# Turning the second expert's rows with VectorE and an exchange of quadrants, in the expert stage of an attention and mixture-of-experts layer

## The reference, cut to what matters

```python
buf = zeros(E * CAP + 1, H).at[slot].set(x[tok])      # E = 32 experts, CAP = 512 rows each
xe = buf[:E * CAP].reshape(E, CAP, H)                 # H = 256
gu = einsum('ech,eoh->eco', xe, gate_up_proj)         # 128 gate and 128 up columns
g, u = minimum(gu[..., :I], 7), clip(gu[..., I:], -7, 7)
h = silu(g) * u
ye = einsum('eci,ehi->ech', h, down_proj)             # gathered later, eight rows a token
```

## Time and profile before

| | |
|---|---|
| median of 3 runs | 3135.45 us (3132.16 to 3135.75) |
| the profiled execution's own time | 3129.23 us |
| its span, from first to last instruction | 3127.6 us |
| expert stage: first transpose to the first scores of the attention | 555.3 to 764.5 us |
| PE busy over the span | 98% |
| mean granted TensorE clock | 0.995 of full speed |

### The profile page before, as it was taken

The page is one execution under the profiler, slowest core; times in us unless marked ns, Lnnn a source line. Parts: engine busy times, 40 slices in busy tenths (PEclk is TensorE's granted clock), DMA queues, the critical chain, the costliest instruction groups (busy, mean ns, idle before and its releaser), DMA issues.

```text
span 3127.6 us, 54519 instructions
## 1 busy us (share of the span) xinstructions
PE 3068.8 (98%) x13443; PEld 1592.7 (51%) x13444; DVE 2624.5 (84%) x2773; ACT 1963.5 (63%) x3797; POOL 2102.4 (67%) x2156
## 2 busy tenths in 40 slices
PE   8999999999899999999999999999999999999998
PEld 3355444555455555555555555555555555555554
DVE  9622444334999999999999999999999999999995
ACT  5511420334677777777777777777777777777775
POOL 5877773011577777777777777777777777777776
PEclk9999999999999999999999999999999999999999
DMA  9821887665888888898888888988898888888887
GB/s 350 331 88 55 310 266 179 204 228 187 229 205 219 217 223 221 220 221 225 218 218 217 219 216 213 262 219 223 220 223 219 221 219 224 211 220 220 206 215 182
DMA packets 319034, 685.21 MB, mean 219 GB/s; under 512 B 120813, under 2 KB 170744, under 8 KB 318608
## 3 DMA queue, kind: packets, MB, share of 16 engines
q1 hardware_dynamic: 289808, 626.48, 76.0%
q0 software_dynamic: 29184, 58.22, 5.8%
HBM read 198.37 MB, written 159.51 MB: 114 GB/s over the span
## 4 chain that ended last, share of the span: by engine, by line
PE 69%; DMA 2%; SPq 2%; DVE 1%; issue 0%; ACT 0%; POOL 0%; DVEq 0%; ACTq 0%; POOLq 0%
PE ea_ps L1155 28%; PE ea_ps L1187 26%; PE ea_ps L1202 9%; PE ea_ps L1168 6%; DMA ea_moved<-ea_blocks 2%; SPq L976 1%; DVE ea_half_max L1282 1%; DVE ea_blocks L1299 1%; DMA out<-ahead_acc 0%; SPq L819 0%; ACT ea_scaled L1249 0%; ACT ea_prob L1237 0%; SPq L826 0%; SPq L959 0%; DVE ea_neg_max L1287 0%
## 5 line engine op out<-in xcount | busy, mean ns | idle before, releaser
L1237 ACT ACTIVATE ea_prob<-ea_ps,ea_neg_max 128x1024 f32<-128x1024 f32 x1024 | 1149.1, 1122 | 313.8 <-DVE ea_neg_max L1287 292.4
L1282 DVE TENSOR_REDUCE ea_half_max<-ea_ps 128x1 f32<-128x1024 f32 x1024 | 1201.8, 1215 | 8.5 <-PE ea_ps L1155 7.4
L1299 DVE STREAM_TRANSPOSE ea_blocks<-ea_prob 128x1792 f32<-128x1792 f32 x512 | 1043.1, 2037 | 2.9 <-DMA ea_moved<-ea_blocks 1.2
L1093 POOL COPY ea_moved<-ea_blocks 32x1792 f32<-32x1792 f32 x512 | 857.1, 1674 | 158.5 <-DVE ea_blocks L1299 49.0
L1155 PE MATMUL ea_ps<-ahead_k_hl,ahead_q_hh 128*128 128x512 f32 x2048 | 852.9, 416 | 12.7 <-ACT ea_prob L1237 12.2
L1187 PE MATMUL ea_ps<-ea_moved,ea_v 128*64 128x512 f32 x3584 | 860.0, 593 | 5.3 <-DMA ea_moved<-ea_blocks 5.2
L1155 PE MATMUL ea_ps<-ahead_k_hl,ahead_q_ll 128*128 128x512 f32 x2048 | 807.5, 394 | 0.0
L1108 POOL TENSOR_TENSOR ahead_acc<-ahead_acc,ea_scaled 128x256 f32<-128x256 f32 x512 | 375.8, 734 | 203.3 <-ACT ea_scaled L1249 67.4
L1249 ACT ACTIVATE ea_scaled<-ea_ps,ea_inv 128x256 f32<-128x256 f32 x512 | 242.2, 473 | 316.8 <-PE ea_ps L1202 312.0
L1187 PEld LDWEIGHTS ea_ps<-ea_moved,ea_v 128*64 128x64 f32 x3584 | 261.7, 137 | 351.9 <-issue 292.9
L1155 PEld LDWEIGHTS ea_ps<-ahead_k_hl,ahead_q_hh 128*128 128x128 f32 x2048 | 387.6, 189 | 85.5 <-ACT ea_prob L1237 19.5
(11 more groups left out here) (112 smaller groups left out, 2563.6 us busy)
## 6 DMA issues: line engine op xcount, KB each, us to landing
ea_moved<-ea_blocks SPq DMA_DIRECT2D x1536, 224.0 KB, 6.2
ahead_k_hl<-k_parts SPq DMA_DIRECT2D x64, 512.0 KB, 8.1
ahead_q_hh<-q_parts SPq DMA_DIRECT2D x128, 256.0 KB, 4.6
ahead_q_ll<-q_parts SPq DMA_DIRECT2D x128, 256.0 KB, 5.7
xbuf<-pr_zeros SPq DMA_DIRECT2D x32, 512.0 KB, 3.8
q_parts<-pr_part_hi SPq DMA_DIRECT2D x64, 256.0 KB, 2.4
q_parts<-pr_part_lo SPq DMA_DIRECT2D x64, 256.0 KB, 2.5
k_parts<-pr_part_hi SPq DMA_DIRECT2D x64, 256.0 KB, 2.4
```

The source lines that it names most:

```text
L1093: nc.gpsimd.tensor_copy(moved[r * 32:(r + 1) * 32, parity, r, :, :, :], blocks[r * 32:(r + 1) * 32, parity, r, :, :, :]).then_inc(diag_don ...
L1237: nc.scalar.activation(prob[:, i % 2, half * 1024:(half + 1) * 1024], ps[:, banks[0]:banks[1], :].rearrange("p b c -> p (b c)"), ACT.Exp, ...
L1282: nc.vector.tensor_reduce(half_max[:, i % 2, half:half + 1], ps[:, banks[0]:banks[1], :], AX.XY, ALU.max).then_inc(max_step, 1)
L1299: nc.vector.transpose(blocks[:, parity, :, j, :, :].rearrange("p c t k -> p t c k"), prob[:, (s["s"] - 1) % 2, 0:MOVED * P].rearrange("p ( ...
```

## The change

Of each pair only the first expert (`q` = 0) is still turned by PE. The second one's rows are turned by DVE in blocks of 32 x 32 (`turn_second`) into a new tile `blk`, from which twelve transfers issued by SP (`exchange`) and four copies on POOL (`diagonal`) bring the blocks into `xeT`. `blk` and `xeT` have two buffers each (`b`); the rows of the second expert are loaded two pairs ahead, those of the first one pair ahead. `load_expert` is split into `load_rows` and `load_weights`. A partition now holds four consecutive tokens (`(p t) d` in place of `(t p) d`), in the load of rows and in the store of `ye`. The loops are unrolled over two pairs, with two pairs written out at either end. The order on SP:

```diff
-                load_expert(sp, io, scr, ahead, e, q)
-        for part in range(2):
-            load_k(sp, scr, start, 0, 0, 0, part)
-        load_q(sp, scr, start, 0, 0, 0)
-        with sp.Fori(1, E // 2) as i:
-            load(i)
+        def exchange(i, b):
+            wait_apart(sp, blk_done, i + 1, sp_waits)
+            wait_apart(sp, gu_ready, 2 * (i - 1), sp_waits)
+            for turn in range(1, QD):
+                for a, r in zip(ACROSS, ACROSS[turn:] + ACROSS[:turn]):
+                    sp.dma_start(xeT[r * 32:(r + 1) * 32, b, a, :, :, :],
+                                 blk[a * 32:(a + 1) * 32, b, r, :, :, :]).then_inc(exchanged[b], 16)
+        def body(i, b):
+            if follows(i, 2):
+                wait_apart(sp, blk_done, i + 2, sp_waits)
+                load_rows(sp, scr, ahead, i + 2, 1)
+            if follows(i, 1):
+                exchange(i + 1, 1 - b)
+                wait_apart(sp, turned, i + 1, sp_waits)
+                load_rows(sp, scr, ahead, i + 1, 0)
+                for q in range(2):
+                    wait_apart(sp, gu_ready, 2 * i + q + 1, sp_waits)
+                    wait_apart(sp, dn_kept, 2 * i + q + 1, sp_waits)
+                    load_weights(sp, io, ahead, 2 * i + 2 + q, q)
+        sp.wait_ge(blk_done, 1)
+        load_rows(sp, scr, ahead, 1, 1)
+        exchange(0, 0)
+        for part in range(2):
+            load_k(sp, scr, start, 0, 0, 0, part)
+        load_q(sp, scr, start, 0, 0, 0)
+        over_pairs(sp, body)
```

The other engines, cut to what changes:

```diff
     def gpsimd(pool):
+        def diagonal(i, b):
+            wait_apart(pool, blk_done, i + 1, pool_waits)
+            wait_apart(pool, gu_ready, 2 * (i - 1), pool_waits)
+            for r in range(QD):
+                nc.gpsimd.tensor_copy(xeT[r * 32:(r + 1) * 32, b, r, :, :, :],
+                                      blk[r * 32:(r + 1) * 32, b, r, :, :, :]).then_inc(diag_done, 1)
...
     def vector(dve):
+        def turn_second(i, b):
+            dve.wait_ge(xe_loaded[1], 16 * i + 16)
+            if not isinstance(i, int) or i > 1:
+                dve.wait_ge(exchanged[b], SENT // 2 * (i - b))
+                dve.wait_ge(diag_done, QD * (i - 1))
+            nc.vector.transpose(blk[:, b, :, :, :, :].rearrange("p r t k j -> p (t k) r j"),
+                                xe[:, 1, :, :].rearrange("p t (k r j) -> p (t k) r j", r=QD, j=32)).then_inc(blk_done, 1)
...
+        def body(i, b):
+            hidden(i, 0)
+            if follows(i, 2):
+                turn_second(i + 2, b)
+            hidden(i, 1)
+        for i in range(2):
+            turn_second(i, i)
+        over_pairs(dve, body)
...
     def tensor(pe):
+        def gate_up(i, q, b):
+            pe.wait_ge(w_loaded[q], 32 * i + 32)
+            if q == 0:
+                pe.wait_ge(xeT_done, i + 1)
+            else:
+                pe.wait_ge(exchanged[b], SENT // 2 * (i - b) + SENT)
+                pe.wait_ge(diag_done, QD * i + QD)
+                    x_T = xeT[:, b, :, :, k, :].rearrange("p a t j -> p t a j") if q else first_T[:, k, :]
...
-        def both(i):
-            for q in range(2):
-                turn(i, q)
-                down(i - 1, q)
-                gate_up(i, q)
+        def body(i, b):
+            turn(i)
+            for q in range(2):
+                if not isinstance(i, int) or i:
+                    down(i - 1, q)
+                gate_up(i, q, b)
...
             if half == 0:
+                if isinstance(tile, int) and tile == 0:
+                    pe.wait_ge(ye_done, E - 1)
```

More of the change, by code:

```diff
@@ L639, in experts_programs @@
     CT = CAP // P
-    xe, gu, dn, loaded = (ahead[name] for name in ("xe", "gu", "dn", "loaded"))
+    PAIRS = E // 2
+    SENT = QD * (QD - 1) * 16
+    xe, gu, dn, xe_loaded, w_loaded = (ahead[name] for name in ("xe", "gu", "dn", "xe_loaded", "w_loaded"))
     room = moved[:, :, :, :, :, :].rearrange("p a r j t k -> p (a r j t k)")
+    size = 2 * QD * CT * DK * 32
     def lines(n):
-        first = n * CAP
+        first = 2 * size + (DK + n) * CAP
         return room[:, first:first + 2 * CAP].rearrange("p (q c) -> p q c", c=CAP)
-    xeT = room[:, 0:2 * DK * CAP].rearrange("p (q k c) -> p q k c", q=2, c=CAP)
-    gate, up, silu_g, hid = (lines(2 * DK + 2 * n) for n in range(4))
-    dn_old = lines(2 * DK + 8)[:, 0, :].rearrange("p (q d) -> p q d", d=D)
+    xeT, blk = (room[:, n * size:(n + 1) * size].rearrange("p (b a t k j) -> p b a t k j", b=2, a=QD, t=CT, k=DK)
+                for n in range(2))
+    first_T = room[:, 2 * size:2 * size + DK * CAP].rearrange("p (k c) -> p k c", c=CAP)
+    gate, up, silu_g, hid = (lines(2 * n) for n in range(4))
+    dn_old = lines(8)[:, 0, :].rearrange("p (q d) -> p q d", d=D)
     ye = start["acc"][:, TILES // 2:, :].rearrange("p (q t) d -> p q t d", q=2)
@@ L655, in experts_programs @@
     xeT_done = m.sem("e_xeT_done")
+    blk_done = m.sem("e_blk_done")
+    exchanged = m.sems("e_exchanged", 2)
+    diag_done = m.sem("e_diag_done")
     gu_ready = m.sem("e_gu_ready")
@@ L662, in experts_programs, with over_pairs, follows @@
     sp_waits, pool_waits = m.sem("e_sp_waits"), m.sem("e_pool_waits")
-    def sync(sp):
-        def load(i):
-            for q in range(2):
[L667 to L670, removed]
-                load_expert(sp, io, scr, ahead, e, q)
+    def over_pairs(eng, body):
+        for i in (0, 1):
+            body(i, i)
+        with nc.Fori(1, PAIRS // 2 - 1, engines=[eng.engine]) as j:
+            for u in range(2):
+                body(2 * j + u, u)
+        for i in (PAIRS - 2, PAIRS - 1):
+            body(i, i % 2)
+    def follows(i, n):
+        return not isinstance(i, int) or i + n < PAIRS
+    def sync(sp):
+        def exchange(i, b):
[20 more added lines that the diff above has]
+        exchange(0, 0)
         for part in range(2):
@@ L704, in silu @@
         def silu(i, q):
-            n = 2 * i + q
[L706 to L711, removed]
-        def both(i):
-            for q in range(2):
-                turn(i, q)
-                down(i - 1, q)
[L717 to L744, removed]
+            act.wait_ge(gate_done, 2 * i + q + 1)
@@ new lines, in silu, with vector, hidden, body @@
+            nc.scalar.activation(silu_g[:, q, :], gate[:, q, :], ACT.Silu).then_inc(silu_done, 1)
+        def body(i, b):
+            take(i)
+            for q in range(2):
+                if not isinstance(i, int) or i:
+                    down(i - 1, q)
+                silu(i, q)
+        over_pairs(act, body)
+        for q in range(2):
+            down(PAIRS - 1, q)
+    def vector(dve):
+        def turn_second(i, b):
[5 more added lines that the diff above has]
+                                xe[:, 1, :, :].rearrange("p t (k r j) -> p (t k) r j", r=QD, j=32)).then_inc(blk_done, 1)
+        def hidden(i, q):
+            n = 2 * i + q
+            dve.wait_ge(gu_ready, n + 1)
+            wait_pos(dve, down_ready, n - 1)
+            nc.vector.tensor_copy(dn_old[:, q, :], dn[:, q, :]).then_inc(dn_kept, 1)
+            nc.vector.tensor_scalar(gate[:, q, :], ps[:, 4 + 2 * q, :], LIMIT, None, ALU.min
+                                    ).then_inc(gate_done, 1)
+            nc.vector.tensor_scalar(up[:, q, :], ps[:, 5 + 2 * q, :], LIMIT, -LIMIT, ALU.min, ALU.max
+                                    ).then_inc(up_done, 1)
+            dve.wait_ge(up_done, n + 1)
+            dve.wait_ge(silu_done, n + 1)
+            nc.vector.tensor_tensor(hid[:, q, :], silu_g[:, q, :], up[:, q, :], ALU.mult
+                                    ).then_inc(hid_done, 1)
+        def body(i, b):
+            hidden(i, 0)
[5 more added lines that the diff above has]
+        over_pairs(dve, body)
@@ L774, in down, with body @@
             last.then_inc(down_ready, 1)
-        for q in range(2):
[L777 to L782, removed]
-                gate_up(i, q)
[L785 to L789, removed]
+        def body(i, b):
+            turn(i)
+            for q in range(2):
+                if not isinstance(i, int) or i:
+                    down(i - 1, q)
+                gate_up(i, q, b)
+        over_pairs(pe, body)
+        for q in range(2):
+            down(PAIRS - 1, q)
     return dict(sync=sync, gpsimd=gpsimd, scalar=scalar, vector=vector, tensor=tensor)
```

53 lines of the change are left out of this document (27 added, 26 removed).

## The result

The changed kernel takes 3176.18 us at the median (3170.18 to 3180.94, 4 runs), against 3135.6 us of the kernel before on the same chip (3132.16 to 3138.44): a ratio of 1.0137, 95% interval 1.0124 to 1.015. It is slower, as forecast, but by 41 us where 22 were forecast; the median lies 1.2 us above the range. The profiled execution took 3170.18 us, with a span of 3168.5.

The account below looks back on a forecast made before the run. PE was taken to bound the kernel, busy 98% of the span. Pairs -15.3 us, the start, seven late turns +18.6 and low clock +6.5 came to +22, 3157 us on the median; range 3145 to 3166, 8 in 10 3130 to 3175.

Parts of the forecast that it names:

- T: Expert stage: PE's time for a pair without the second expert's `turn` and copy wait, 11.63 us against 12.66 before.
- low clock at the start: First pairs of the expert stage: about 9 us of PE idle brings the 1.2 GHz level, costing 3 us.
- seven late turns: Expert stage, pairs 3 to 15: every second `turn` waits 2.7 us for its rows, 18.6 us in sum.
- low clock behind them: After late turns: 1.2 GHz level loses 1.6 us each time, taken for four of seven, +6.5 us.
- Start: Second pair's `turn`: SP's exchanges delay its rows, so it starts at 563.3 + 24d, 578.8 us, against 570.00 before.
- d: SP's queue: cost of one exchange issue with the gap to the next, taken as 0.645 us from the attention's issues.
- X: From a pair's last `gate_up` end to the rows needed one pair later: 6.55 + 12d, 14.3 us against 11.63.
- a wait and the landing of the first expert's rows, 0.15 + 3.75: Last step behind the exchange in SP's sum: 0.15 us wait, then 3.75 us until the rows land.
- more is late than the rows: Rival: d = 0.69, low clock after each late pair, +31 us, 3166; with 5 us landing, 3175; chance 0.10.
- The tail is untouched: After the expert stage: the new `ye_done` wait ahead of the first scores adds nothing, 0 us.
- Cheap issues: Rival: SP's issues at d = 0.378 bring rows in time, -10 us, 3125 on the median; chance 0.12.
- the even case: Rival: d between 0.447 and 0.564 leaves the time within 6.3 us either way; chance 0.18.

Follow-up runs that it names:

- experiment 2: Changed kernel with the twelve exchange transfers kept but each carrying 4 KB instead of 32 KB: one run, 3171.88 us.
- experiment 6: Changed kernel with first expert's rows issued ahead of the exchange, its weights issued by ScalarE, attention's K and Q behind the last pair: 3123.09 us, ratio 0.9974.
- Experiment 5: Changed kernel with 16 unread identity products on PE ahead of every second `turn` from the fourth pair on: 3167.38 us, ratio 1.0108.
- Experiments 7 and 8: Unwaited semaphore additions on POOL: 206 added to the changed kernel, 3171.27 us, ratio 1.0126; 54 added to the kernel before, 3138.33 us, ratio 1.0022.
- experiment 4: Changed kernel with the old `(t p) d` layout in the load of rows and the store of `ye`: one run, 3178.64 us.
- experiment 1: Changed kernel with SP issuing the first expert's rows of the next pair ahead of the twelve exchange transfers: 3146.11 us, ratio 1.0047.

## Why the prediction came out as it did

The direction and the mechanism in the expert stage were right: the place in SP's queue made every second `turn` late. Mis-sized there were the landing of the rows and the low clock behind the waits, and one step, that the attention is untouched, was wrong. Its terms against the profile (each pair's length is the distance of two starts of `turn`; a pair without a wait takes 11.49):

| term, us | predicted | after |
|---|---|---|
| 15 pairs at T, against 189.8 before | -15.3 | 15 x 11.49 - 189.8 = -17.4 |
| second pair's `turn` later | 578.8 - 570.0 = +8.8 | 579.15 - 570.00 = +9.2 |
| low clock at the start | +3 | 13.17 - 11.49 = +1.7 |
| seven late turns | +18.6 | +29.0 |
| low clock behind them | +6.5 | +11.9 |
| last pair of `down` | +22 | +34.3 |
| attention | 0 | +6.6 |

- **What PE loses.** T was put at 11.63 and is 11.49: by subtraction the wait for the copy was worth 0.29 us (12.66 - 0.88 - 11.49), not 0.15. That the strided read of the exchanged tile costs nothing is right, since 11.49 holds the whole pair.
- **Start.** The sum came out, its terms less so: the second exchange took 8.55 us instead of 7.74, the attention's K and Q 2.4 instead of 2.1, and the rows landed after 3.4 instead of 3.8.
- **DVE and POOL.** Forecast 1.2 us and at most a quarter of 1.67 us; measured 1.24 and 0.40, both beside PE's work.
- **The price of an issue.** Forecast d = 0.645 and 7.74 us for twelve; measured in steady state blocks of 7.49 to 8.29 us, 7.74 in the first pair shown. That 32 KB cost what 224 KB cost was the choice on which the sign hung, and experiment 2 carries it down to 4 KB; the attention's 598 ns at the median stand beside 591 here. The Trainium skill ("DMA: Bandwidth & Descriptors", Rules for kernel authors) counts transfers under 64 KB as mostly overhead; by experiment 2 the trace agrees. The Trainium skill's sentence there that the time to initiate a DMA is usually small relative to the DMA (Issuing engines are not separate DMA queues) is no guide for this exchange: 591 ns of issue stand to 2.5 us of landing for each, and twelve issues take two thirds of a pair. The same section of the Trainium skill says that issuing from several engines saves sequencer time alone; the weights that ScalarE issues in experiment 6 are such a saving, and one of its three edits.
- **Steady state: mis-sized.** Every second `turn` is late, seven times, as forecast. From the end of a pair's work (the start of its successor's punctual `turn`) to the late one X was forecast as 14.3 us; the seven are 14.96, 16.36, 15.08, 16.56, 16.21, 15.71 and 14.52, mean 15.63. Of the excess 1.3, the issue of the rows accounts for 0.3 (10.8 us behind that end, where the sum has 10.5), and the step that failed, "a wait and the landing of the first expert's rows, 0.15 + 3.75", for the rest: from issue to `turn` the rows took 4.34, 5.15, 3.79, 5.49, 5.10, 4.77 and 5.06 us, mean 4.8. The estimate that longer runs land a little sooner than 3.9 went the wrong way. With T shorter by 0.14 the lateness is 4.1 us instead of 2.7, and 29.0 in sum. The rival "more is late than the rows" had this landing at 5 us and a low clock behind every late pair, both near what was measured; that its 3175 is closest to the 3176 measured is partly luck, since it has all of its 40 us in the expert stage, where 34.3 arose.
- **Low clock: mis-sized.** "I take four of seven": it was all seven, at 1.7 us each where 1.6 was forecast. Experiment 5 shows that the loss goes with the idle time and not with the late rows as such.
- **"The tail is untouched": wrong.** The reason given, that the new wait ahead of the first scores asks for nothing new, was true and did not cover what happened. The attention lost 6.6 us because POOL's pause fell on a gather. Experiments 7 and 8 bring that about and undo it with instructions that have nothing to do with the change. No row of before priced it, but the pause itself stood in its trace, 4.16 us ahead of an addition.
- **The other rivals.** Cheap issues and the even case asked for d under 0.564; no block of the exchange in steady state has under 7.49 / 12 = 0.62. The exchange is never late for PE, nor is DVE.

**Open.** Why the rows land later behind the exchange: the layout (experiment 4) doesn't account for it and the bytes for little (in experiment 2, with an eighth of them, the rows of the late turns still took 4.5 us on average from issue to `turn`, against 4.8), and with the rows ahead of the exchange, where they are under way together with it, they land later still (6.2 us at the median in experiment 1). Why the expert stage starts at 554.9 to 555.3 us in four kernels and at 557.1 to 558.3 in the other seven, each profiled once, whose first parts are the same but for added semaphore instructions or none: this is 2.8 us that moves with no edit that I can name. That POOL's pause is the loading of its next instructions fits with its moving by the program's length and with the packet of the instruction queue in each; but the profile does not say whose instructions the packet brought, nor that POOL waited for it, so this stays argued.

## What to carry to other kernels

Work taken from the engine that sets the pace comes back through the queue that has to feed it: count a pair's issues by their number, set that sum against the pair's length, and look at what stands last in the queue, for that is what will be late. A short wait on TensorE costs more than itself where the clock drops behind it, so give the queue to the operands of the next product first, and let another engine issue what SP has no time for. Before a small difference far from the edit is explained by the edit, change the length of the programs alone and see whether it moves.

## What the runs showed of the hardware

- An issue of a transfer from SBUF to SBUF over 32 partitions costs SP 591 ns at the median for 4 KB and for 32 KB, and 598 for 224 KB; a load of 128 partitions mostly 330 to 360.
- POOL has a pause of 4.2 to 5.0 us in the attention whose place goes with the length of its program (52 instructions more by the page's count moved it in the kernel before, 204 more in the changed one), with one packet of the instruction queue in each. Ahead of an addition it costs nothing that shows; ahead of a gather it costs PE 5 to 6 us of a 73-us window, and the kernel 7.
- In the changed kernel all seven idle times of 2.9 to 4.9 us on PE were followed by eight transposes in 1.97 us instead of 1.04, at 0.50 in the window shown, the 1.2 GHz level, with 1.3 to 2.5 us lost each time.
